# A graph layer on one Trainium2 core: first tiles loaded singly, a norm and part of a fold moved among products, and the feed-forward pass reordered

## What is computed

```python
xn = _layernorm(x, axis=-1)
x = x + gnn(xn, W, edge_weight, src, dst) + mix(xn[None], Wq, bq, Wk, bk, Wv, bv, weights)[0]
x = x + ffn(_layernorm(x, axis=-1)[None], w_gate, w_up, w_down)[0]
```

## Time and profile before

| | us |
|---|---|
| median of 3 runs | 1732.07 |
| the profiled execution | 1732.95 |
| its span | 1730.1 |
| PE busy in the span | 1671.7 (97%) |
| DVE busy | 1096.4 (63%) |
| POOL busy | 585.3 (34%) |
| ACT busy | 521.7 (30%) |

### The profile page before, as it was taken

How to read it: one execution, slowest core, us unless ns; L and a number is a source line. 1 busy time by engine, 2 the same in 40 slices (tenths; PEclk the granted TensorE clock), 3 DMA queues, 4 the chain that set the end, 5 groups by cost and what they waited for, 6 DMA issues and landing times.

```text
span 1730.1 us, 23534 instructions
## 1 busy us (share of the span) xinstructions
PE 1671.7 (97%) x8070; PEld 1350.5 (78%) x8070; DVE 1096.4 (63%) x2542; ACT 521.7 (30%) x619; POOL 585.3 (34%) x392
## 2 busy tenths in 40 slices
PE   5899999999999999999999999999999999998897
PEld 5799988877888888888877777787877878875565
DVE  6776554466667866656666664485674865846764
ACT  4442310322222111114222222233332333333443
POOL 2011566787776777777667100000000000000000
PEclk9999999999999999999999999999999999999999
DMA  9998988445686765557877646245345453453455
GB/s 298 355 401 324 315 243 254 119 99 112 161 199 164 201 141 136 137 155 182 239 206 205 182 151 198 91 136 141 95 137 137 141 140 92 143 134 94 138 160 165
DMA packets 159268, 307.99 MB, mean 178 GB/s; under 512 B 60386, under 2 KB 95250, under 8 KB 159208
## 3 DMA queue, kind: packets, MB, share of 16 engines
q1 hardware_dynamic: 89572, 227.66, 41.8%
q0 software_dynamic: 61824, 52.62, 14.8%
...
## 4 chain that ended last, share of the span: by engine, by line
PE 91%; DVE 4%; DMA 2%; ACT 1%; issue 1%; ACTq 0%; SPq 0%; DVEq 0%
PE PS L363 23%; PE PS L364 23%; PE PS L362 23%; PE PS L1347 4%; PE PS L1348 4%; PE PS L1349 4%; PE PS L1557 4%; PE PS L1582 2%; PE PS L1407 2%; DMA xnT<-XT 1%; DMA Aside<-A_dense 1%; DVE stats L976 1%; ACT hqT L942 1%; PE PS L1364 0%; PE PS L1327 0%
## 5 line engine op out<-in xcount | busy, mean ns | idle before, releaser
L695 POOL DMA_INDIRECT A_dense<-wtot,cell x336 | 542.2, 1614 | 225.1 <-DMA A_dense<-wtot,cell 133.5
L363 PE MATMUL PS<-SH,AL 125*125 125x512 f32 x784 | 309.6, 395 | 0.0
L364 PE MATMUL PS<-SH,AH 125*125 125x512 f32 x784 | 309.4, 395 | 0.0
L362 PE MATMUL PS<-SL,AH 125*125 125x512 f32 x784 | 307.9, 393 | 0.2 <-DVE AL L1183 0.2
L362 PE MATMUL PS<-WL,xtH 128*125 128x512 f32 x640 | 252.6, 395 | 0.0
L363 PE MATMUL PS<-WH,xtL 128*125 128x512 f32 x640 | 251.7, 393 | 0.0
L364 PE MATMUL PS<-WH,xtH 128*125 128x512 f32 x640 | 251.3, 393 | 0.0
L1181 DVE TENSOR_TENSOR SL<-S,SH 125x1024 fp32r<-125x1024 f32 x98 | 119.9, 1223 | 167.3 <-ACT SH L879 167.3
L879 ACT ACTIVATE SH<-S 125x1024 fp32r (+1 forms) x98 | 103.9, 1061 | 317.1 <-PE PS L364 317.1
L362 PEld LDWEIGHTS PS<-SL,AH 125*125 125x125 f32 x784 | 145.4, 185 | 38.8 <-DVE AL L1183 1.6
L363 PEld LDWEIGHTS PS<-SH,AL 125*125 125x125 f32 x784 | 145.7, 186 | 36.4
...
## 6 DMA issues: line engine op xcount, KB each, us to landing
...
```

Source lines behind the costliest of these rows:

```text
L362: nc.tensor.matmul(o, lh, rl, start=start, stop=False)
L363: nc.tensor.matmul(o, ll, rh, start=False, stop=False)
L364: return nc.tensor.matmul(o, lh, rh, start=False, stop=stop)
L695: pool.indirect_dma_start(cells[m], bass.IndirectOffsetOnAxis(cell[:, col:col + 1], 0), wtot[:, col:col + 1], None, compute_op=ALU.add).th ...
```

## The change

- SP loads tiles 0 and 1 each by itself, then pair 1, then the edge lists; pairs 3 to 9 wait for the sums of the pair three before. POOL's strip r waits for min(4r, 20) tiles.
- DVE and ACT treat tiles 0 and 1 singly, in a new order; the edge keys come after tile 2's low part; ACT runs one square root on a constant before the first rows.
- In q's last step DVE weighs q's right banks before the low part of Wk's last rows and the last edge pair. q's sum, norm and scaled map are made during k's products (one PE matmul after k's third step). The fold is cut by matrix: q's halves of its first two blocks stand ahead of k's scaled map. It turns over three pairs of banks instead of two. The bias is folded once, from a broadcast operand, straight into all partitions; L817 and L1422 go.
- In the feed-forward pass the input transposes of tiles 0 and 1 go into banks 0 and 4, tile 0's within the last aggregation step, before its last row tile. The hidden transposes stand inside `gate_up` after 12 of its 16 matmuls. Half of the last group's row sums go ahead of the first hidden rows. The rounding of the last four tiles is split in two (`largest_r`, `round_r`, together `quantise_r`) and spread over tiles 3 to 12. The last two tiles leave out what nobody uses. The last tile is added and written in two halves, and the two unused loads go.

```diff
+NORM_BANK = (5, 1)
+X_BANK = (0, 4)
+ROUNDED_AT = (4, 6, 9, 12)
...
-load_pair(0)
+for t in range(2):
+    split_rows(sp, X[:, t, :], x[t * ROWS:(t + 1) * ROWS, :], (s_x[0], s_second)[t])
+load_pair(1)
...
 for p in range(3, NP):
+    sp.wait_ge(s_st, 2 * (p - 2))
     load_pair(p)
...
-with sp.Fori(0, HALF) as h:
+with sp.Fori(0, HALF - 1) as h:
     for i in range(2):
         t = h * 2 + i
         sp.wait_ge(s_z[i], HALF + h + 1)
         split_rows(sp, out[bass.ds(t * ROWS, ROWS), :], fin[:, i, :], s_uout[i])
-        load_r((t + 2) % TILES, i)
-for i in range(2):
-    sp.wait_ge(s_zx[i], ZX_END + 32 * (HALF + 1))
-    sp.wait_ge(s_uout[i], 32 * HALF)
+        load_r(t + 2, i)
+sp.wait_ge(s_z[0], 2 * HALF)
+split_rows(sp, out[NODES - 2 * ROWS:NODES - ROWS, :], fin[:, 0, :], s_uout[0])
+for c in range(2):
+    cols = slice(c * 512, (c + 1) * 512)
+    sp.wait_ge(s_z[1], 2 * HALF + c)
+    split_rows(sp, out[NODES - ROWS:NODES, cols], fin[:, 1, cols], s_uout[1])
+sp.wait_ge(s_uout[0], 32 * HALF)
+sp.wait_ge(s_uout[1], 32 * (HALF + 1))
...
-        pool.wait_ge(s_gm, min(3 * r, TILES))
+        pool.wait_ge(s_gm, min(4 * r, TILES))
...
-deviations(0)
+nc.scalar.activation(norms[:, 7, 0:1], eps[:, :], ACT.Sqrt)
+deviations(0, 1)
 high_of_rows(0)
+deviations(1, 2)
 for n in range(TILES):
+    if n == 0:
+        high_of_rows(1)
     if n % 2 == 0 and n + 2 < TILES:
-        deviations(n // 2 + 1)
-    high_of_rows(n + 1)
+        deviations(n + 2, n + 4)
+    if n:
+        high_of_rows(n + 1)
     transposed_rows(n)
...
+def norm_of(m):
+    act.wait_ge(s_norm, 6 * m + 2)
+    nc.scalar.activation(norms[:, 1, m:m + 1], PS[:, NORM_BANK[m], 0:1], ACT.Sqrt).then_inc(s_norm, 1)
+
+norm_of(0)
...
-nc.scalar.activation(norms[:, 7, 0:1], eps[:, :], ACT.Sqrt)
-act.wait_ge(s_norm, 2)
-nc.scalar.activation(norms[:, 1, :], PS[:, 1, 0:2], ACT.Sqrt).then_inc(s_norm, 1)
+norm_of(1)
 for k in range(KT):
     act.wait_ge(s_fold, k + 1)
-    nc.scalar.activation(TH[:, k, :], two_banks(2 + k % 2), ACT.Copy).then_inc(s_fh, 1)
+    nc.scalar.activation(TH[:, k, :], two_banks(1 + k % 3), ACT.Copy).then_inc(s_fh, 1)
...
-act.wait_ge(s_fold, KT + 1)
-nc.scalar.activation(brow[0:1, :], two_banks(2)[0:1], ACT.Copy).then_inc(s_bb, 1)
...
+nc.scalar.activation(norms[:, 7, 0:1], eps[:, :], ACT.Silu)
+transposed_x(0, 0, X_BANK[0])
+transposed_x(1, 0, X_BANK[1])
 act.wait_ge(s_fb, 1)
-transposed_x(0, 0)
 silu_gate(0, 0, 0)
-transposed_x(1, 0)
-ffn_tile(0, 0)
-deviation(GROUPS - 1)
-for d in range(1, GT):
-    ffn_tile(d // 2, d % 2)
-    integers(GROUPS - 1, d - 1)
-integers(GROUPS - 1, GT - 1)
-act.wait_ge(s_fb, 2)
-with act.Fori(GT // 2, HALF) as h:
-    for i in range(2):
-        ffn_tile(h, i)
+for t in range(TILES):
+    if t == TILES - GT - 1:
+        act.wait_ge(s_fb, 2)
+    ffn_tile(t // 2, t % 2, min(2, TILES - 1 - t))
+    if t == 1:
+        deviation(GROUPS - 1)
+    if t in ROUNDED_AT:
+        integers(GROUPS - 1, ROUNDED_AT.index(t))
...
-row_sums(0)
-for p in range(NP):
-    normalise(p)
-    if p == 0:
+row_sums(0, 1)
+normalise(0, 1)
+row_sums(1, 2)
+low_of_rows(0)
+normalise(1, 2)
+low_of_rows(1)
+row_sums(2, 4)
+for a in range(2, TILES, 2):
+    normalise(a, a + 2)
+    if a == 2:
+        low_of_rows(2)
         edge_keys()
-    if p + 1 < NP:
-        row_sums(p + 1)
-    for t in range(2 * p, 2 * p + 2):
+    if a + 2 < TILES:
+        row_sums(a + 2, a + 4)
+    for t in range(a + (a == 2), a + 2):
...
+def sum_of_parts(m):
+    dve.wait_ge(s_bs, (m + 1) * NB)
+    dve.wait_ge(s_rs, 2)
+    nc.vector.tensor_reduce(norms[:, 0, m:m + 1], parts[:, m, :], AX.X, ALU.add).then_inc(s_norm, 1)
+
+def scaled_maps(m):
+    total, n = PS[:, NORM_BANK[m], 0:1], 6 * m
+    dve.wait_ge(s_norm, n + 3)
+    nc.vector.reciprocal(norms[:, 2, m:m + 1], norms[:, 1, m:m + 1]).then_inc(s_norm, 1)
+    dve.wait_ge(s_norm, n + 4)
+    for half in (slice(0, KT // 2), slice(KT // 2, KT)):
+        nc.vector.tensor_scalar(bdqk[m][:, half].rearrange("p k n -> p (k n)"),
+                                bd[:, half].rearrange("p k n -> p (k n)"),
+                                norms[:, 2, m:m + 1], None, ALU.mult).then_inc(s_bdq, 1)
+    nc.vector.tensor_tensor(norms[:, 3, m:m + 1], total, norms[:, 2, m:m + 1], ALU.mult).then_inc(s_norm, 1)
+    dve.wait_ge(s_norm, n + 5)
+    nc.vector.tensor_tensor(norms[:, 3, m:m + 1], norms[:, 3, m:m + 1], norms[:, 2, m:m + 1],
+                            ALU.mult).then_inc(s_norm, 1)
+
+for j in range(KT - 1):
     low_of_weights(1, j)
     edges(STEP_Q + KT + j)
 weigh(0, 1)
+low_of_weights(1, KT - 1)
 for m in range(2):
     nc.vector.scalar_tensor_tensor(squares[:, m], bias[:, m, :, 0], float(NODES), bias[:, m, :, 0], ALU.mult, ALU.mult,
                                    accum_out=parts[:, m, NB:NB + 1]).then_inc(s_rs, 1)
+sum_of_parts(0)
+edges(STEP_Q + 2 * KT - 1)
 for j in range(KT):
+    if j == 4:
+        scaled_maps(0)
     edges(STEP_K + j)
 weigh(1, 0)
...
-dve.wait_ge(s_bs, 2 * NB)
-dve.wait_ge(s_rs, 2)
-nc.vector.tensor_reduce(norms[:, 0, :], parts[:, :, :], AX.X, ALU.add).then_inc(s_norm, 1)
...
+sum_of_parts(1)
+scaled_maps(1)
...
+def add_last_down():
+
+    dve.wait_ge(s_uout[1], (HALF - 1) * 32)
+    dve.wait_ge(s_zx[1], ZX_END + HALF * 32)
+    for c in range(2):
+        cols = slice(c * 512, (c + 1) * 512)
+        dve.wait_ge(s_u[1], HALF + c)
+        nc.vector.scalar_tensor_tensor(fin[0:ROWS, 1, cols], PS[0:ROWS, 4 + c, :], h_sc[0:ROWS, 1, 2:3],
+                                       rt[0:ROWS, 1, cols], ALU.mult, ALU.add).then_inc(s_z[1], 1)
...
 add_z(GROUPS - 1)
+row_stats(GROUPS - 1, ORDER[:2])
 dve.wait_ge(s_fb, 1)
 hidden(0, 0)
-row_stats(GROUPS - 1, ORDER)
+row_stats(GROUPS - 1, ORDER[2:])
 row_moments(GROUPS - 1)
-hidden(0, 1)
-inverse_deviation(GROUPS - 1)
-quantise_r(GROUPS - 1, 0)
-add_down(0, 0)
-hidden(1, 0)
-quantise_r(GROUPS - 1, 1)
-add_down(0, 1)
-hidden(1, 1)
-quantise_r(GROUPS - 1, 2)
-add_down(1, 0)
-quantise_r(GROUPS - 1, 3)
-dve.wait_ge(s_rq[1], TILES // 2)
+for t in range(1, TILES - GT - 2):
+    hidden(t // 2, t % 2)
+    add_down((t - 1) // 2, (t - 1) % 2)
+    if t == 2:
+        inverse_deviation(GROUPS - 1)
+    if t + 1 in ROUNDED_AT:
+        largest_r(GROUPS - 1, ROUNDED_AT.index(t + 1))
+    if t in ROUNDED_AT:
+        round_r(GROUPS - 1, ROUNDED_AT.index(t))
+dve.wait_ge(s_f6, TILES * 4 - 1)
 scales_back(slice(TILES - GT, TILES))
 dve.wait_ge(s_fb, 2)
-with dve.Fori(GT // 2, HALF) as h:
+with dve.Fori((TILES - GT - 2) // 2, HALF) as h:
     hidden(h, 0)
     add_down(h - 1, 1)
     hidden(h, 1)
     add_down(h, 0)
-add_down(HALF - 1, 1)
+add_last_down()
...
+def total_of(m):
+    pe.wait_ge(s_norm, 6 * m + 1)
+    nc.tensor.matmul(PS[:, NORM_BANK[m], 0:1], earlier[:, 0, :], norms[:, 0, m:m + 1], start=True,
+                     stop=True).then_inc(s_norm, 1)
+
 for m in range(2):
     for right in range(2):
+        if m and right:
+            pe.wait_ge(s_norm, 5)
         for j in range(KT):
             pe.wait_ge(s_lo, G_ITEMS + m * KT + j + 1)
             gram(2 + 2 * m + right, split[:, j, 0], split[:, j, 1], j == 0, j == KT - 1)
-
-pe.wait_ge(s_norm, 1)
-nc.tensor.matmul(PS[:, 1, 0:2], earlier[:, 0, :], norms[:, 0, :], start=True, stop=True).then_inc(s_norm, 1)
-
-def fold(lhs_of, rows, slot):
+            if m and not right and j == 2:
+                total_of(0)
+
+def fold(k, m):
     for j in range(KT):
-        if rows == P and slot == 0:
-            pe.wait_ge(s_bdq, 4 if j >= KT // 2 else 2)
+        if k == 0:
+            pe.wait_ge(s_bdq, 2 * m + 1 + j // (KT // 2))
+        last = nc.tensor.matmul(by_block(two_banks(1 + k % 3))[:, j, :], raw[:, m * KT + j, k * P:(k + 1) * P],
+                                bdqk[m][:, j, :], start=m == 0 and j % (KT // 2) == 0, stop=m == 1,
+                                skip_group_check=True)
+    if m:
+        last.then_inc(s_fold, 1)
+
+pe.wait_ge(s_bs, 2 * NB - 5)
+fold(0, 0)
+total_of(1)
+fold(1, 0)
+fold(0, 1)
+fold(1, 1)
+for k in range(2, KT):
+    if k >= 3:
+        pe.wait_ge(s_fl, k - 2)
+    for m in range(2):
+        fold(k, m)
+
+def map_of_bias():
+    for j in range(KT):
         for m in range(2):
-            last = nc.tensor.matmul(by_block(two_banks(2 + slot))[0:rows, j, :], lhs_of(m * KT + j), bdqk[:, m, j, :],
-                                    start=m == 0, stop=m == 1)
-    last.then_inc(s_fold, 1)
-
-for k in range(KT):
-    if k == 1:
-        pe.wait_ge(s_norm, 5)
-    if k >= 2:
-        pe.wait_ge(s_fl, k - 1)
-    fold(lambda n: raw[:, n, k * P:(k + 1) * P], P, k % 2)
-pe.wait_ge(s_fl, KT - 1)
-fold(lambda n: raw[:, n, D:EXT], 2, 0)
-pe.wait_ge(s_fl, KT)
-pe.wait_ge(s_bb, 1)
-for c in range(2):
-    last = nc.tensor.matmul(PS[:, 6 + c, :], earlier[0:1, 0, :], brow[0:1, c * 512:(c + 1) * 512], start=True, stop=True)
-last.then_inc(s_bb, 1)
+            last = nc.tensor.matmul(by_block(two_banks(3))[:, j, :], bias[:, m, j, 0:1].to_broadcast([P, P]),
```

(101 more changed lines are left out.)

81 lines of the change are left out of this document (38 added, 43 removed).

## The result

The changed kernel takes 1679.69 us (median of 4 runs, 1679.44 to 1679.91), beside 1733.52 for the kernel before in the same comparison (4 runs, 1731.98 to 1737.02). The ratio is 0.9687, 95% interval 0.967 to 0.9703. The forecast was 1685.0, with a range of 1677 to 1697. The span fell from 1730.1 to 1677.7, by 52.4 where 47.1 were forecast.

| up to | us won, forecast | us won, measured | difference |
|---|---|---|---|
| a product behind the fold (343.23, now 317.07) | 22.7 | 26.2 | +3.5 |
| last row tile of the aggregation (1574.76, now 1550.13) | 22.7 | 24.6 | +1.9 |
| first `gate_up` (1577.48, now 1551.29) | 23.5 | 26.2 | +2.7 |
| first down product (1587.43, now 1560.36) | 24.4 | 27.1 | +2.7 |
| fifth down product (1625.72, now 1583.96) | 38.3 | 41.8 | +3.5 |

A forecast was written before the change was run, and what follows sets the result against it. PE, busy for 97% of the span, was taken as the bound. Start 9.4, q to fold 13.3 and feed-forward 24.4 sum to 47.1 us: 1732.95 becomes 1685.9, with the median 0.9 below at 1685.0; range 1677 to 1697.

The forecast's parts named there:

- rival 6: Start: no stall left and an earlier first tile, better than forecast at 1680 us; chance 0.09.
- Term A: Start and gram left: earlier first tile and paced loads win 3.3 + 8.6 - 2.5 = 9.4 us.
- The start's 3.3: Start: PE reaches the transposes behind tile 3 at 29.3 instead of 32.71, 3.3 us won.
- the residue of 2.5: Gram left: of the 8.6 us stall behind a late transposed-tile write, 2.5 us stay; bounds 0 and 8.6.
- Rival 1: Start gives little: low clock at PE's wait for tile 3's low part, 3 to 9 us more, say 1693; chance 0.20.
- Term B: q, k and the fold: pauses and low clock go, 3.9 + 2.6 + 5.6 + 1.6 - 0.4 = 13.3 us won.
- rival 3: Fold: k's chain not hidden (2.9 + 1.6 us) or broadcast operand loaded slowly (3.6); 1689 to 1693; chance 0.08.
- whatever is won before them moves them as they are: Products and aggregation, 336 to 1575 us: left alone by the change, they keep all earlier gains.
- Term C: Feed-forward: earlier start, spread roundings, shorter tiles and shorter tail win 24.4 us.
- the 1.7 taken off the last steps: Last feed-forward tiles: 0.5 us less for input transposes left out, 1.2 less in the last without `gate_up`.
- Rival 2: Feed-forward: DVE becomes the bound, split roundings uncovered and the 0.24 us wait unhidden; 1690 to 1693; chance 0.12.
- Rival 4: POOL takes over: later strips delay the scatters by more than 25 us; up to 1708; chance 0.02.

## Why the prediction was right, point by point

The three terms err on the same side, so the 1679.7 came out beside rival 6's 1680 and not beside the forecast's 1685. Two more steps of the sum cancelled by luck: a run was put at 2.85 above its span and took 1.7, and the median was put at 0.9 below the profiled run and lay 0.25 above it.

**Term A: 9.4 forecast, 11.8 measured**, and 10.4 in the changed kernel's second profile. The start's 3.3 came as 3.1: first sums at 4.88 for 5.2, tile 3's products at 26.3 for 26.7. The step that failed is the residue of 2.5: "the phase still needs nearly all of the bandwidth ... 385 GB/s against the 366 seen". I took a rate seen in a jam for the engines' limit. The same engines gave 395 and 419 GB/s later in the stage, and 420 even in the jam of the kernel before, from 60 to 63 us. Nothing of the stall was left in the first profile, 1.3 us in the second (pairs 7.41 and 7.67 apart at its end). The Trainium skill (DMA: Bandwidth & Descriptors, Queues, rings and completion order) has the engines go round the queues packet by packet, and the prediction drew from it that nothing of the stall would be left. The first profile agrees with that, and so does the pacing tested alone; the second keeps 1.3 us and a wait of ACT of 3.07 for a write. Rival 6 had both of its conditions here: no stall, and a first tile 0.3 earlier. They make 2.8 of the 5.3 by which the forecast was off.

**Rival 1** was a real mechanism with a wrong price. The low clock behind the wait for tile 3 is missing in the changed kernel's profiles and stands in eight others with this start, where it costs 1.1 us on the chain, not "3 us more": DVE, not PE, sets the pace just behind it. I gave it one chance for the whole kernel; it comes and goes from one execution to the next.

**Term B: 13.3 forecast, 14.3 measured**, in both profiles of the changed kernel (26.2 at the product behind the fold, less A's 11.8; in the second 24.77 less 10.45). Up to k's last product it is 297.21 - 278.92 - 11.8 = 6.4, where 3.9 + 2.6 - 0.4 = 6.1 were summed. From there to the first product with the folded matrix it is 6.3 for 5.6: a block takes 3.57 instead of 3.60, and the norm matmul takes 0.14 of PE's time, not 0.4. The clock behind the fold gave the 1.6 that were forecast. There is no pause before the fold, the bias map has a block's price, and q's norm makes no wait. The 2.6 for the clock in front of k rest on one draw too: it was low for 6.8 us there, but for 3.4 in the kernel before with the pacing alone, behind the same wait of 3.94. The exposed chain costs 4.0, near the 2.9 + 1.6 of rival 3, so that rival had its price and not its way. As to "the 2.9 us around the norm matmul ... were not [followed by the low clock]": that holds in all three profiles with the old chain, but 2.0 us of waits at the same place were followed by it with the fold behind.

**Between B and C**, "whatever is won before them moves them as they are" failed for the aggregation, by 1.1 us: 0.9 of it are PE's longer waits for `AL`. These waits differ between executions (0.2 to 2.7 us in all, over the fourteen profiles), so how much of it the change brought is open.

**Term C: 24.4 forecast, 27.4 measured** (52.4 less the 24.6 up to the aggregation's last row tile and the 0.4 of transposes ahead of it). Up to the fifth down product it is 16.7 for 15.6, and the fifteen steps behind it gave 7.8, not 5.2, both in the main by the same step. That is "the last 0.24 is the wait for the copy of the hidden transposes", so 6.06: a tile takes 5.85, since a wait costs PE also the overlap of the two instructions that it parts. 19 such steps of 0.21 are 4.0 us. The Trainium skill (TensorE: Matmul & The Clock Gate, Step-by-step: what each phase is for) has the drain of one matmul overlap the fill of the next; an overlap of 0.16 in the record is in line with that. Against it, the 1.7 taken off the last steps came as 1.1. The tail is the part that came out short: 7.1 behind the last down product's start, not 6.3. The fixed part was smaller than the 3.7 I took (2.8 from the last addition's end to the end), but I carried 1.9 for a product that stood behind two waits of 2.17 and 0.68, and it took 3.55. **Rival 2** did not come: neither DVE nor ACT ends a wait in tiles 4 to 12, while the roundings packed into neighbouring tiles did bring it out.

**Rival 4** came nearer than I put it. "Their end at 956.19" is the start of the last scatter, and was one draw: over the thirteen later profiles, the last scatter begins anywhere from 952.85 to 969.29, and the first load of A follows 12 to 34 us behind it. Where the traces have its landing, it comes 3 to 5.5 us behind the start. The strips' pacing does not show in it. The cover held, but by these figures a kernel some 7 to 9 us faster up to this point (an estimate) would have to watch POOL.
